# Last cross attention: K and V of batch 0 moved behind the last expert tile, gates and part of a quantisation moved into the expert stage

## Chip, cores and metric

One core of one Trainium2 chip runs the whole program. The metric is the time of one execution on the device, in microseconds (us); of several executions the median is given. A row of the trace gives a start and a duration from the first instruction of the profiled execution.

## What is computed

The reference is two transformer layers over 32 batches of 112 rows of 256 numbers, with a context of 375 rows of 192 numbers per batch:

```python
x = x + L0_xattn(layernorm(x), ctx)   # 16 heads of 16
x = x + L0_ffn(layernorm(x))          # self attention, then a mixture of 8 experts, 2 per row
x = x + L1_xattn(layernorm(x), ctx)   # 8 heads of 64
x = x + L1_ffn(layernorm(x))          # row blocks of 32 rounded to a 6-bit grid, times a rounded 256x256 weight
```

The part that matters here is where the experts end and the third line begins. Each row is sent to its two best experts, `moe_out = g0*y0 + g1*y1`, and the two gates are a softmax of the two best router logits, so `g0 = 1/(1+r)` and `g1 = r/(1+r)` with `r = exp(top1 - top0)`. In the last cross attention `k = ctx @ Wk` and `v = ctx @ Wv` need the context and the weights alone, while `q = layernorm(x) @ Wq` needs x, with the experts' result in it.

## The kernel before

The program has four parts that run one after the other on all engines: `cross_first`, `self_attention`, `experts`, `cross_last`. Every engine has its own list of instructions, in an order written out by hand, and waits on semaphores; the lists of the parts follow one another without a barrier.

**Experts (lines 1230 to 1450).** The rows were scattered by expert into `slots` in device memory, in 63 tiles of 128 rows (`MOE_TILES`). For each tile, SP loads `xg` and the first weight; TensorE turns `xg` (L1431), forms `hidden` (16 matmuls, L1423) and later the result `ps_out` (24 matmuls, L1443); ScalarE applies Gelu (L1338) and rounds the activations (`e_aH`, L1343) and the second weight (`e_w2H`, L1330); VectorE forms the low halves `e_aL` (L1394) and `e_w2L` (L1369, two halves) and adds the bias (`e_y`, L1389); SP stores `e_y` to `slots` (L1307). TensorE's order in step t is: hidden of t, turn of t+1, result of t-1. VectorE's order is: `e_xT` of t+1, `e_y` of t-1, `e_aL` and both halves of `e_w2L` of t.

In the step of the last tile VectorE also runs the first 3 of 13 steps (`EARLY`) that round the last weight `e_wf` (function `quantise_steps`, L1207 to L1222), and the other 10 behind the last `e_y`.

**Preparation in the expert stage.** In step 1, SP loads the contexts of batches 0 and 1, and the weights of `cross_last` (`preload`). ScalarE rounds Wk and Wv (L1524, L1526). GpSimd (POOL) splits the context of batch 0 into `c_cH` (L1576) and `c_cL` (L1582), and the low parts of Wk and Wv (L1592 to L1600). It then waits for the last store of the experts, and fetches the two expert rows of each row of batch 0 with two indirect DMAs into `c_got` (`fetch`, L1557 to L1567).

**Last cross attention (lines 1453 to 2142).** `step(b)` is written once per engine and unrolled for the first batches, then looped (`over_batches`, L56). The units in TensorE's order are: turn of the normalised rows `c_xn` (L1889), scores of head pairs 0 and 1 (L102, three split matmuls per head), q of the next batch (L1874), scores 3 and 2, values (L114) of the batch before, K of the next batch (four products of five matmuls, L182), V of this batch (three products of five), and turns of the probabilities (L108). Each K product goes through ScalarE twice (copy `c_kT`, rounded `c_kH`), and through GpSimd once (`c_kL`). VectorE mixes the expert rows into x (`mix`, L1774), takes moments (L155, L158), GpSimd forms the inverse deviation (L162, L164), and VectorE applies it (`c_xn`, L169). On VectorE the order is: mix of batch n, apply of batch n-1, moments of batch n.

At the start of this part VectorE and ScalarE form the gates (L1756 to L1762 and L1649). SP, in its step b (L1534 to L1544), waits until the context of batch b is split (`c_split`), then loads the context of batch b+2; in steps 0, 1 and 2 it also brings a third of the `residual` rows that were lent to the experts back from device memory (L1541).

`experts` calls, all in hand-written order:

```python
quantise = quantise_steps(dve, link, wf, wf, mx, 2 * D // MX, 128)
EARLY = 3
```

## Time and profile before

| what | value |
|---|---|
| median of 3 runs | 1969.74 us (1966.71 to 1970.39) |
| profiled execution, its own time | 1969.25 us |
| span of its instructions | 1967.4 us |
| outside the span | 1.85 us |
| TensorE busy | 1872.3 us (95%) |
| VectorE, ScalarE, GpSimd busy | 1495.6, 1270.8, 953.1 us |
| mean granted TensorE clock | 0.977 |
| expert stage | about 848 to 1288 us |
| last cross attention | about 1288 us to the end |

A view of the trace is read by time: a row has a start, a duration, the engine, the line of the kernel, `out<-in`, and in square brackets how long that engine was idle before it, and which instruction ended the idle time. PEld is TensorE's loading of weights, SPq and POOLq are queues that issue DMAs. In a table of stretches, each engine has its busy time and its count of instructions, and then come granted clock (1.00 is 2.4 GHz, 0.50 is 1.2 GHz), the DMA engines' mean share and GB/s.

### The profile page before, as it was taken

The numbers are of one execution on the slowest core, as the hardware profiler recorded it, in microseconds if no ns is written. First come the engines' busy times: TensorE is split into PE (matmuls) and PEld (weight loads), VectorE is DVE, ScalarE is ACT, GpSimd is POOL, SyncE is SP. The second block draws the span as 40 slices with busy tenths as digits, with TensorE's granted clock in tenths as the row PEclk, the third lists the DMA queues.
The fourth block names the chain that finished last, engine by engine and source line by source line (L and its number), as shares of the span: only waits on it lengthen the run. The fifth ranks groups of instructions, "written<-read, shape, count | busy, mean of one in ns | idle before, by whom it ended". The sixth has DMA issues, their size and how long they took to land.

```text
span 1967.4 us, 61539 instructions
## 1 busy us (share of the span) xinstructions
PE 1872.3 (95%) x20887; PEld 1642.5 (83%) x20887; DVE 1495.6 (76%) x3438; ACT 1270.8 (65%) x2720; POOL 953.1 (48%) x1616
## 2 busy tenths in 40 slices
PE   7999999999699999879999999969999999999996
PEld 5888888888578788679999999958888888888885
DVE  6778878887278887756766666657888888888886
ACT  2555555555377777657777777747777777777773
POOL 4566556655246766640000000057766767676751
PEclk9999999999799999889999999979999999999998
DMA  8222332231050111165565555421111111111100
GB/s 236 90 88 87 109 95 87 87 111 40 1 182 28 37 40 36 61 237 190 187 202 197 188 205 194 160 82 55 36 41 34 40 34 30 42 32 40 34 15 10
DMA packets 116596, 182.05 MB, mean 93 GB/s; under 512 B 10851, under 2 KB 94563, under 8 KB 116067
## 3 DMA queue, kind: packets, MB, share of 16 engines
q1 hardware_dynamic: 110386, 166.51, 26.6%
q0 software_dynamic: 6144, 14.69, 2.5%
q8 instruction: 40, 0.66, 0.1%
q14 instruction: 26, 0.21, 0.0%
HBM read 127.68 MB, written 53.48 MB: 92 GB/s over the span
## 4 chain that ended last, share of the span: by engine, by line
PE 52%; DVE 2%; issue 1%; ACT 1%; POOL 1%; DMA 0%; DVEq 0%; ACTq 0%; POOLq 0%; SPq 0%
PE ps_quad L1423 11%; PE ps_out L1443 9%; PE ps_quad L182 6%; PE ps_quad L102 4%; PE ps_out L114 4%; PE ps_turned L108 4%; PE ps_quad L1874 3%; PE ps_turned L182 3%; PE ps_proj L1894 3%; PE ps_proj L182 2%; PE ps_proj L1899 1%; DVE c_negmax L119 1%; PE ps_proj L1431 1%; ACT c_probs L134 0%; DVE e_w2L L1369 0%
## 5 line engine op out<-in xcount | busy, mean ns | idle before, releaser
L1423 PE MATMUL ps_quad<-e_xT,w 128*128 128x128 f32 x2016 | 235.3, 275 | 1.7 <-DVE e_xT L1381 1.7
L1423 PEld LDWEIGHTS ps_quad<-e_xT,w 128*128 128x128 f32 x2016 | 230.4, 192 | 2.2 <-DVE e_xT L1381 2.2
L364 ACT ACTIVATE a_probsT<-ps_quad 125x1792 f32<-125x1792 f32 x96 | 159.9, 1666 | 100.6 <-PE ps_quad L533 100.6
L1563 POOL TENSOR_TENSOR c_held<-minus_half 1x1 f32<-1x1 f32 x32 | 9.4, 294 | 410.8 <-DMA slots<-e_y 408.3
L1338 ACT ACTIVATE e_act_T<-ps_quad,fc_b 128x128 f32<-128x128 f32 x504 | 137.3, 384 | 94.2 <-PE ps_quad L1423 94.2
L134 ACT ACTIVATE c_probs<-ps_quad,c_negmax 112x375 f32<-112x375 f32 x256 | 143.8, 572 | 64.6 <-DVE c_negmax L119 64.6
L1443 PE MATMUL ps_out<-e_w2H,e_aH 128*128 128x256 f32 x504 | 149.1, 296 | 8.9 <-DVE e_w2L L1369 8.9
L126 DVE TENSOR_SCALAR c_probs<-c_probs,c_recip 112x375 f32<-112x375 f32 x256 | 151.5, 632 | 4.5
L1369 DVE TENSOR_TENSOR e_w2L<-w,e_w2H 128x1024 fp32r<-128x1024 f32 x126 | 151.4, 1243 | 0.0
L421 DVE TENSOR_REDUCE a_negmax<-ps_turned 112x2 f32<-112x750 f32 x128 | 120.1, 938 | 34.2 <-PE ps_turned L519 34.0
L119 DVE TENSOR_REDUCE c_negmax<-ps_quad 112x2 f32<-112x750 f32 x128 | 113.9, 930 | 40.0 <-PE ps_quad L102 39.5
L1443 PE MATMUL ps_out<-e_w2L,e_aH 128*128 128x256 f32 x504 | 143.1, 284 | 0.0
L1443 PE MATMUL ps_out<-e_w2H,e_aL 128*128 128x256 f32 x504 | 142.8, 283 | 0.0
L419 DVE TENSOR_REDUCE a_negmax<-ps_quad 112x4 f32<-112x1500 f32 x64 | 110.2, 1722 | 36.3 <-PE ps_quad L519 36.3
L1330 ACT ACTIVATE e_w2H<-w 128x1024 fp32r x126 | 125.6, 1042 | 2.5 <-PE ps_out L1443 2.5
L1389 DVE TENSOR_TENSOR e_y<-ps_out,e_b 128x256 f32<-128x256 f32 x63 | 26.7, 425 | 109.5 <-PE ps_out L1443 109.5
L1443 PEld LDWEIGHTS ps_out<-e_w2H,e_aH 128*128 128x128 f32 x504 | 97.0, 192 | 12.2 <-issue 6.1
L108 PEld LDWEIGHTS ps_turned<-ident,c_probs 112*125 112x125 f32 x768 | 100.9, 188 | 7.5 <-issue 2.4
L108 PE MATMUL ps_turned<-ident,c_probs 112*125 112x112 f32 x768 | 103.8, 271 | 1.8 <-ACT c_probsT L130 1.8
L130 ACT ACTIVATE c_probsT<-ps_turned 125x672 f32<-125x672 f32 x128 | 95.1, 743 | 10.6 <-PE ps_turned L108 8.2
L359 ACT ACTIVATE a_kT<-ps_proj,a_bk 128x376 f32<-128x376 f32 x64 | 36.8, 575 | 100.5 <-PE ps_proj L182 100.5
L1394 DVE TENSOR_TENSOR e_aL<-e_act_T,e_aH 128x1024 fp32r<-128x1024 f32 x63 | 78.3, 1243 | 30.3 <-issue 26.6
(350 smaller groups left out, 6025.1 us busy)
## 6 DMA issues: line engine op xcount, KB each, us to landing
w<-in_fc_t SPq DMA_DIRECT2D x71, 1024.0 KB, 4.9
slots<-a_zeros SPq DMA_DIRECT2D x60, 512.0 KB, 4.9
a_cT<-in_ctx_t SPq DMA_DIRECT2D x32, 375.0 KB, 3.5
c_cT<-in_ctx_t SPq DMA_DIRECT2D x32, 375.0 KB, 3.2
e_xg<-slots SPq DMA_DIRECT2D x63, 128.0 KB, 3.9
slots<-e_y SPq DMA_DIRECT2D x63, 128.0 KB, 1.8
out<-c_fo SPq DMA_DIRECT2D x32, 112.0 KB, 1.9
residual<-in_x SPq DMA_DIRECT2D x1, 2912.0 KB, 20.7
```

What stands on the lines that cost most here:

```text
L108: last = pe.transpose(self.turned[:, j, c * T:(c + 1) * T], self.probs[u][:, j, c * self.chunk:(c + 1) * self.chunk], ident[0:T, 0:T])
L119: dve.tensor_reduce(self.negmax[:, u, :], self.scores[u % 2], AX, ALU.max, negate=True).then_inc(self.max_ready, 1)
L126: last = dve.tensor_scalar(p, p, self.recip[:, u, j:j + 1], None, ALU.mult)
L134: last = act.activation(self.probs[u][:, j, :], self.scores[u % 2][:, j, :], ACT.Exp, bias=self.negmax[:, u, j:j + 1], accum_out=self.sums ...
L182: last = pe.matmul(dst, left, right, start=(i == 0), stop=(i == len(terms) - 1))
L364: act.activation(probsT[:, 2 * i:2 * i + 2, :, :].rearrange("p c r x -> p r c x"), quad[0:KC, :, 0:2 * HALF].rearrange("p r (c x) -> p r c ...
L421: dve.tensor_reduce(rows[:, 2 * half:2 * half + 2, 0], plain[0:T, :, 0:CTX], AX, ALU.max, negate=True)\
L1330: act.activation(w2H[:, half * HALF:(half + 1) * HALF], weights_half(e, half), ACT.Copy).then_inc(w2_high, 1)
L1338: last = act.activation(act_T[par][:, c * TILE:(c + 1) * TILE], hidden[par][:, c // 4, (c % 4) * TILE:(c % 4 + 1) * TILE], ACT.Gelu, bias= ...
L1369: dve.tensor_tensor(w2L[:, half * HALF:(half + 1) * HALF], weights_half(e, half), w2H[:, half * HALF:(half + 1) * HALF], ALU.subtract)\
L1423: last = pe.matmul(hidden[par][:, c // 4, (c % 4) * TILE:(c % 4 + 1) * TILE], mem["w1"][:, par, k, c * 128:(c + 1) * 128], xT[par][:, k, : ...
L1443: last = pe.matmul(y_ps[:, 0:D], left[:, rows], right[:, cols], start=(c == 0 and i == 0), stop=(c == NCH - 1 and i == 2))
```

## The change

Gates: the difference is taken before the first expert tile, and the three operations behind the exponential sit behind the first `e_xT`. Quantisation: `EARLY = (4, 7)`: four steps go ahead of the second-last `e_y`, three follow the last `e_w2L`, six stay behind the last `e_y`. K and V of batch 0: all seven products are issued behind the last expert result, before the turn of `e_wf`; ScalarE handles them in `first_products`; GpSimd forms the low parts in `first_low`, and splits the context of batch 1 in the expert stage. `later(b)` removes the same work for batch 0 from `step`. SP's list isn't edited.

```diff
 # experts, scalar
+                act.wait_ge(gap, 1)
+                act.activation(ratio[:, :], ratio[:, :], ACT.Exp).then_inc(ratioed, 1)
...
 # experts, vector
+                dve.tensor_tensor(ratio[:, :], mem["top"][:, :, 1], mem["top"][:, :, 0], ALU.subtract).then_inc(gap, 1)
...
-                EARLY = 3
+                EARLY = (4, 7)
...
+                    if isinstance(t, int) and t == MOE_TILES - 1:
+                        dve.wait_ge(bias_in, 32)
+                        for action in quantise[:EARLY[0]]:
+                            action()
                     if exists(t - 1, MOE_TILES):
...
+                    if isinstance(t, int) and t == -1:
+                        gates()
                     if isinstance(t, int) and t == MOE_TILES - 1:
-                        dve.wait_ge(bias_in, 32)
-                        for action in quantise[:EARLY]:
+                        for action in quantise[EARLY[0]:EARLY[1]]:
                             action()
...
 # cross_last
+        later = lambda b: not (isinstance(b, int) and b == 0)
...
 # cross_last, gpsimd
                 pool.wait_ge(v_split, 2)
+                context_high(1, 1)
+                context_low(1, 1)
                 index_rows(0, 0)
                 for i, tiles in enumerate(((MOE_TILES + 1) // 2, MOE_TILES // 2)):
                     pool.wait_ge(mem["y_out"][i], 16 * tiles)
                 fetch(0, 0)
+                fetch(1, 1)
+
+                def first_low(of):
+                    pool.wait_ge(k_high, 4)
+                    for tile in of:
+                        pool.tensor_tensor(kL[0][:, tile, :], kT[:, tile, :], kH[0][:, tile, :], ALU.subtract).then_inc(k_ready, 1)
+
+                first_low((0, 1))
...
                     if exists(b + 3):
                         norm.pool_rstd(pool, b + 3)
+                    if isinstance(b, int) and b + 3 == 0:
+                        first_low((3, 2))
...
 # cross_last, scalar
-                act.wait_ge(gap, 1)
-                act.activation(ratio[:, :], ratio[:, :], ACT.Exp).then_inc(ratioed, 1)
+                act.activation(unit[:, :], mem["eps"][:, :], ACT.Exp)
+                def first_products():
+                    k_from = (psum["turned"][:, 1, :], psum["quad"][:, 2, :], psum["quad"][:, 3, :], psum["turned"][:, 0, :])
+                    for at, tile in enumerate((0, 3)):
+                        act.wait_ge(k_mm, at + 1)
+                        act.activation(kT[:, tile, :], k_from[tile][:, 0:CTXE], ACT.Copy).then_inc(k_whole, 1)
+                    act.wait_ge(k_whole, 1)
+                    act.activation(kH[0][:, 0, :], kT[:, 0, :], ACT.Copy).then_inc(k_high, 1)
+                    act.wait_ge(v_mm, 1)
+                    act.activation(v[0][:, 2, :], proj[0:KC, 0:INNER], ACT.Copy).then_inc(v_ready, 1)
...
 # cross_last, vector
-                dve.tensor_tensor(ratio[:, :], mem["top"][:, :, 1], mem["top"][:, :, 0], ALU.subtract).then_inc(gap, 1)
...
-                dve.tensor_tensor(mem["gates"][1][:, :], mem["gates"][0][:, :], ratio[:, :], ALU.mult).then_inc(gated, 1)
...
 # cross_last, tensor
+                pe.wait_ge(c_split, 2)
+                pe.wait_ge(mem["experts_xT"], MOE_TILES)
+                pe.wait_ge(mem["experts_h"], MOE_TILES)
+                k_product(psum["turned"][:, 1, :], 0, 0)
+                k_product(psum["turned"][:, 0, :], 0, 3)
+                pe.wait_ge(v_split, 2)
+                v_product(proj, 0, 2)
+                k_product(psum["quad"][:, 3, :], 0, 2)
+                k_product(psum["quad"][:, 2, :], 0, 1)
+                v_product(psum["quad"][:, 0, :], 0, 0)
+                v_product(psum["quad"][:, 1, :], 0, 1)
                 pe.wait_ge(mem["last_y"], MOE_TILES)
                 pe.wait_ge(mem["wf_ready"], 1)
...
+                pe.wait_ge(v_ready, 3)
```

GpSimd's list behind the split of the weights, before and then after. `c_got` is filled by `fetch`, `c_kL` is the low half of K, `c_norm_rstd` the inverse deviation of the rows of one batch.

```order
L1600 TENSOR_TENSOR c_wvH<-c_wv,c_wvH 64x512
L1554 COPY c_index<-slot 112x1 x2
L1563 TENSOR_TENSOR c_held<-minus_half 1x1
L1565 DMA c_got<-slots,c_index 112x256 x2
...
L162 TENSOR_TENSOR c_norm_rstd<-c_norm_moments,eps 112x1
L164 TENSOR_TENSOR c_norm_rstd<-c_norm_rstd,minus_half 112x1
...
L1629 TENSOR_TENSOR c_qL<-c_qT,c_qH 128x448
L1634 TENSOR_TENSOR c_kL<-c_kT,c_kH 128x376
```

```order
L1620 TENSOR_TENSOR c_wvH<-c_wv,c_wvH 64x512
L1594 TENSOR_TENSOR c_held<-minus_half 1x1
L1596 CAST c_cH<-c_cT 128x376 x2
L1602 TENSOR_TENSOR c_cL<-c_cT,c_cH 128x376 x2
L1574 COPY c_index<-slot 112x1 x2
...
L1633 TENSOR_TENSOR c_kL<-c_kT,c_kH 128x376 x2
L162 TENSOR_TENSOR c_norm_rstd<-c_norm_moments,eps 112x1
L164 TENSOR_TENSOR c_norm_rstd<-c_norm_rstd,minus_half 112x1
L1633 TENSOR_TENSOR c_kL<-c_kT,c_kH 128x376 x2
```

The split of batch 1's context now stands ahead of the wait for the experts' last store, and two of the four low halves of K stand ahead of the first inverse deviation, the other two ahead of the fetch for batch 2.

TensorE's list from the last expert matmul on, before and then after. `ps_turned` and the first `ps_quad` rows are K, `c_wvH` marks V, `e_wf` is the last weight, `c_wq` is q.

```order
L1443 MATMUL ps_out<-e_w2H,e_aL_52 128x256
...
L1857 MATMUL ps_out<-ident,e_wf 128x128 x4
L1889 MATMUL ps_proj<-ident,c_xn 128x112 x2
L1874 MATMUL ps_quad<-c_xT,c_wq 128x112 x8
L182 MATMUL ps_turned<-c_cH,c_wkH 128x376
L182 MATMUL ps_turned<-c_cL,c_wkH 128x376
```

```order
L1463 MATMUL ps_out<-e_w2H,e_aL_52 128x256
...
L182 MATMUL ps_turned<-c_cH,c_wkH 128x376
L182 MATMUL ps_turned<-c_cL,c_wkH 128x376
...
L182 MATMUL ps_quad<-c_wvH,c_cL 125x512
L1954 MATMUL ps_out<-ident,e_wf 128x128 x4
L1926 MATMUL ps_proj<-ident,c_xn 128x112 x2
L1911 MATMUL ps_quad<-c_xT,c_wq 128x112 x8
```

The 35 matmuls of K and V stand before the turn of `e_wf`; in the stage of the first two batches they are gone.

## Rows read from the trace of the kernel before

**Rows 1.** Table of stretches: busy time and count by engine, clock, DMA share, GB/s.

```profile
868.00:882.00 14.00, 10.71 (x91) 10.04 (x90) 11.68 (x10) 9.57 (x19) 12.97 (x13) 1.00 0.80 267
...
1288.00:1300.00 12.00, 1.08 (x4) 0.73 (x5) 10.37 (x26) 0.83 (x2) 7.62 (x13) 0.58 0.55 158
...
1334.00:1352.00 18.00, 18.00 (x157) 16.31 (x151) 9.89 (x29) 13.68 (x35) 12.26 (x20) 1.00 0.29 87
```

**Rows 2.** Timeline of TensorE from the last expert tile to batch 1.

```profile
1295.08 1.08 PE L1857 MATMUL ps_out<-ident,e_wf 128*128 128x128 f32 x4 [7.32 <-DVE e_wf L1222]
1300.01 0.61 PE L1889 MATMUL ps_proj<-ident,c_xn 112*128 112x112 f32 x2 [3.85 <-DVE c_xn L169]
1301.07 3.75 PE L1874 MATMUL ps_quad<-c_xT,c_wq 128*128 128x112 f32 x16 [0.45 <-ACT c_xT L1750]
...
1309.43 0.43 PE L102 MATMUL ps_quad<-c_kH,c_qH 64*112 64x376 f32 x2
...
1312.61 0.43 PE L102 MATMUL ps_quad<-c_kH,c_qH 64*112 64x376 f32 x2 [2.41 <-POOL c_kL L1640]
...
1313.32 3.35 PE L1874 MATMUL ps_quad<-c_xT,c_wq 128*128 128x112 f32 x16
...
1323.39 0.47 PE L182 MATMUL ps_quad<-c_wvH,c_cH 128*125 128x512 f32 x1
...
1325.78 0.81 PE L108 MATMUL ps_turned<-ident,c_probs 112*125 112x112 f32 x6
...
1329.87 2.01 PE L1874 MATMUL ps_quad<-c_xT,c_wq 128*128 128x112 f32 x16 [1.00 <-ACT c_probs L134]
```

**Rows 3.** Timeline of VectorE around the mix of the first batches.

```profile
1296.32 1.13 DVE L1774 SCALAR_TENSOR_TENSOR residual<-c_got,gate,residual 112x256 f32<-112x256 f32 x2 [0.20 <-DMA c_got<-slots,c_index]
...
1299.06 0.48 DVE L1774 SCALAR_TENSOR_TENSOR residual<-c_got,gate,residual 112x256 f32<-112x256 f32 x1 [0.56 <-DMA c_got<-slots,c_index]
...
1304.57 0.41 DVE L169 TENSOR_SCALAR c_xn<-residual,c_norm_moments,c_norm_rstd 112x256 f32<-112x256 f32 x1
```

**Rows 4.** The first indirect DMA for batch 0, on GpSimd, and its landing.

```profile
L1565 POOL DMA_INDIRECT c_got<-slots,c_index x1: 1383/1383/1383, 1290.8 to 1290.8; - x1
...
DMA to landing us min/median/max: 5.4/5.4/5.4
```

**Rows 5.** The second indirect DMA for batch 1, on GpSimd, and its landing.

```profile
L1565 POOL DMA_INDIRECT c_got<-slots,c_index x1: 937/937/937, 1296.4 to 1296.4; - x1
...
DMA to landing us min/median/max: 2.6/2.6/2.6
```

**Rows 6.** Waits of SP's DMA queue from 1250 to 1330 us: total, times, longest.

```profile
SPq L1537 <- POOL c_cL L1582: 27.4, 1, 27.4
```

**Rows 7.** Timeline of GpSimd: low halves of q and of K, and both halves of a context.

```profile
1306.09 1.15 POOL L1629 TENSOR_TENSOR c_qL<-c_qT,c_qH 128x448 fp32r<-128x448 f32 x1 [2.82 <-ACT c_qH L1686]
...
1312.59 0.93 POOL L1576 CAST c_cH<-c_cT 128x376 fp32r<-128x376 f32 x2
1313.49 0.97 POOL L1610 TENSOR_TENSOR c_kL<-c_kT,c_kH 128x376 fp32r<-128x376 f32 x1
...
1315.37 1.91 POOL L1582 TENSOR_TENSOR c_cL<-c_cT,c_cH 128x376 fp32r<-128x376 f32 x2
```

**Rows 8.** Timeline of ScalarE in the first batches.

```profile
1311.88 0.57 ACT L134 ACTIVATE c_probs<-ps_quad,c_negmax 112x375 f32<-112x375 f32 x1
...
1318.70 0.58 ACT L134 ACTIVATE c_probs<-ps_quad,c_negmax 112x375 f32<-112x375 f32 x1 [0.84 <-DVE c_negmax L119]
...
1322.58 0.61 ACT L1718 ACTIVATE c_v<-ps_proj 125x512 f32<-125x512 f32 x1
...
1323.66 0.73 ACT L130 ACTIVATE c_probsT<-ps_turned 125x672 f32<-125x672 f32 x1
```

**Rows 9.** Timeline of VectorE in the first expert tiles, with and without GpSimd at work.

```profile
869.82 5.55 DVE L1369 TENSOR_TENSOR e_w2L<-w,e_w2H 128x1024 fp32r<-128x1024 f32 x2
...
887.30 2.35 DVE L1369 TENSOR_TENSOR e_w2L<-w,e_w2H 128x1024 fp32r<-128x1024 f32 x2
```

98 lines of the change are left out of this document (55 added, 43 removed).

## The prediction

> **What bounds the kernel now.** I read the table of stretches first, then TensorE's timeline through the border between the experts and the last cross attention, and then for each gap on TensorE the engine that ended it. In the expert stage and from 1334 us on TensorE is busy all the time: 18.00 of 18.00 us in the stretch from 1334 to 1352 [rows 1]. So time is won or lost only where TensorE stands idle, or runs at its lower clock, and the border is such a place: between 1288 and 1300 it is busy for 1.08 of 12.00 us [rows 1].
>
> Who ends these gaps? The first one, 7.32 us, ends when the last step of the quantisation has written `e_wf`; but behind the four short turns of `e_wf` TensorE waits again, 3.85 us, for `c_xn` of batch 0 [rows 2]. So the quantisation isn't the limit: `c_xn` is. VectorE's order is mix of batch 1, then apply of batch 0, and that mix ended its wait at 1299.06 on a gather [rows 3], which had been issued at 1296.4 and took 2.6 us to land [rows 5]. The front end of the stage is thus a chain of store, four gathers on GpSimd one after the other, mix, apply, turn at 1300.01, q at 1301.07. Behind it the pipeline fills: scores of batch 0 start at 1309.43, the second pair waits 2.41 us for a low half of K from GpSimd and starts at 1312.61, q of batch 1 starts at 1313.32, V has TensorE from 1323.39 to the turn at 1325.78, and q of batch 2 starts at 1329.87 [rows 2]. Behind that TensorE is full, and what is won until then stays won.
>
> **The change, part by part.** I say what each part does to the start of that last turn of batch 0 (1325.78, "the second turn"), because from there on the order of the work is the same.
>
> *Gates and quantisation: nothing.* They leave VectorE's list in front of the first mix, but that mix ended its wait on a DMA at 1296.32 [rows 3]: the gather for it was issued at 1290.8 and took 5.4 us, to 1296.2 [rows 4]. The gather covers them. If that cover were gone, the mix of batch 1 would still wait for its own gather. The four steps that now stand ahead of the second-last `e_y`, and the gates at the start, fall into VectorE's waits there; I put 0 on them.
>
> *K and V of batch 0 behind the last expert tile: cheap where they go.* Of the 35 matmuls, ten of V take 2.39 us [rows 2]; K's have fewer columns, so 35 last at most 8.4 us. They fill a gap of 7.32 us and part of the next, and end by about 1296, so the turn of `e_wf` isn't late, and `c_xn` comes long after.
>
> *From the turn to the first scores.* Before, this lasted from 1300.01 to 1309.43, 9.42 us [rows 2]. K is out of it now, but q, its copies on ScalarE and its low half are not: the low half ended at 1306.09 + 1.15 = 1307.24 [rows 7], so 7.2 us remain. Gain 2.2 us. There is a floor under it: the turn of batch 1 stands ahead of the first scores on TensorE, its rows were ready at 1304.57 + 0.41 [rows 3], and GpSimd now has four low halves of K (0.97 each [rows 7]) ahead of the fetch for batch 2. That fetch, and with it these rows, come some 3 us later, at 1308. So the first scores can't start before about 1308.7, whatever q does.
>
> *The gathers get company: a loss of 2.0 us.* SP's list isn't edited, but what it waits for moves. Before, SP stood for 27.4 us until the context of batch 1 was split [rows 6], and only then loaded the next context and brought the second third of `residual` back. Now that split is done in the expert stage, so SP issues both pairs of transfers in one go at about 1289 to 1290. The gathers of batch 0, which ran beside one such pair, took 5.4 us; those of batch 1, which ran beside nothing, 2.6 [rows 4, 5]. The two gathers of batch 1 will now run beside the second pair. The bounds are 0 and 2.8 us; I take 2.0, nearer to the row with company: the first pair kept the gathers until 1296.2, a second pair of the same size is at work for as long again, but the last gather, issued at 1296.4, meets only its second half. The Trainium skill (DMA: Bandwidth & Descriptors, "Queues, rings and completion order") says that a DMA engine takes turns between its queues packet by packet. By that rule the small packets of a gather wait behind one large packet each, for as long as the other queue has any, and the loss would be the whole 2.8.
>
> So `c_xn` of batch 0 is turned at about 1302.0 and the first scores start at 1302.0 + 7.2 = 1309.2, a gain of 0.2 us over 1309.43. The gather and the K work cancel.
>
> *From the first scores to q of batch 1: gain 0.7.* The wait of 2.41 us is gone, since both low halves are there. But q of batch 1 also waits for the exponentials of the first pair, in its place in PSUM. They ended at 1311.88 + 0.57 = 1312.45 [rows 8], 3.0 us behind the start of the scores, and at the lower clock I add 0.3: 1312.5, and with the handover 1312.6, against 1313.32 [rows 2].
>
> *From q of batch 1 to the second turn: gain 2.0 more.* The exponentials of the next pair started at 1318.70, 5.4 us behind q, and the copy of the first turned probabilities at 1323.66, 5.0 us behind that [rows 8]. Of these 5.0 us one copy of V (about 0.5 net of overlap, 0.61 in its row [rows 8]) is gone. So this copy starts at 1312.6 + 5.4 + 4.5 = 1322.4 (rounded down, as VectorE has less company from GpSimd) and ends with its 0.73 at 1323.1. Before, the second turn then had to wait until 1325.78 because V held TensorE; now it starts at 1323.1. In all the ramp gains 2.7 us. Of 7 us of TensorE's work only this much comes back, because ScalarE's chain of copies and exponentials is late next.
>
> *The clock.* q of batch 1 took 3.35 us and q of batch 2 the same work in 2.01 [rows 2]: the first at 1.2 GHz, the second at 2.4 GHz. Before, that q came after a busy stretch with a hole. Now TensorE is idle from about 1296 to 1302, and between the short pieces up to 1312.6, so I expect the lower level for both q products, as before. Were it the higher one, q of batch 1 would give 1.3 us more.
>
> *GpSimd's split of batch 1 in the expert stage: a loss of 0.8 us.* This is the hidden price. It adds 0.93 + 1.91 = 2.8 us of GpSimd work [rows 7], right behind its preparation at 868 to 882. There GpSimd was busy for 12.97 us, VectorE's two `e_w2L` took 5.55 us instead of 2.35 [rows 9], and TensorE was idle for 14.00 - 10.71 = 3.3 us at full clock [rows 1]; TensorE doesn't make that up, as it is the bound there. In proportion, 2.8 us more cost 3.3 / 12.97 x 2.8 = 0.7, and with the small instruction ahead of it 0.8. The bounds are 0 (all of it between VectorE's long instructions) and 2.8 (one for one). The Trainium skill (SBUF — State Buffer, "Who interferes with whom") says that a VectorE instruction with two inputs in SBUF and a GpSimd instruction that reads SBUF exclude each other, each for its whole length. By that rule the two splits and two casts hit only the instructions they meet, one of them off the path, and the sum would be nearer to 0.5.
>
> **Sum.** -2.7 + 0.8 = -1.9 us. The profiled execution took 1969.25 us, 0.49 below the median of 1969.74; its span is 1967.4 and 1.85 lie around it, untouched. From the profiled execution the sum gives 1967.35, from the median 1967.8. I predict the median to move alike: **1967.8 us**.
>
> **Rivals.** What a measurement of this kernel can tell from no change is about 0.2%, 3.9 us: the line is at 1965.8 and at 1973.7.
>
> 1. *The forecast*: the gathers cost what K gives, ScalarE is late next. 1967.8. Chance 0.5.
> 2. *The clock rises early and the gathers aren't disturbed.* The first scores then start at the floor, 1308.7 or earlier by a little, 0.7 us better with the handovers; q of batch 1 runs at 2.4 GHz, 1.3 us better; the expert stage loses nothing, 0.8 us better. That is -4.7 us: 1965.0. For it speaks that K and V keep TensorE busy up to 1295; against it the hole of 6 us behind. If VectorE, with fewer waits on the port, is also faster in the ramp, it goes lower. Chance 0.22.
> 3. *The expert stage is hit one for one, slower than before.* GpSimd's extra instructions come just as VectorE wants `e_aL` and the first `e_w2L`, on which TensorE waits. Price up to 2.8 us; with the gathers at their full 2.8 (0.8 more than in the sum) the total is -2.7 + 2.8 + 0.8 = +0.9 us: 1970.6. The point from which it decides: 2.7 us lost on TensorE between 880 and 895. `e_w2L` at more than twice its length [rows 9] speaks for it; against it, that only two of its instructions are long. To be slower by over 0.2% it takes a stall that hits several tiles. Chance 0.13.
> 4. *The change takes nothing off the path.* The two low halves ahead of the first inverse deviation, and the fetch behind the other two, make GpSimd the bound of the fill, and the second turn stays where it was. Then only the 0.8 remains: 1970.5. For it speaks that GpSimd has hardly a pause there in the old order [rows 7]; against it, that 2.8 us of splitting leave that same stretch. Chance 0.15.
>
> **Numbers.** The range should leave 2 in 10 out: from case 2, 1965.0, less 0.6 for it going lower, to case 3, 1970.6, with 0.2 for the spread of runs: 1964.4 to 1970.8. Faster by over 0.2% is most of case 2 and the lucky end of case 1: 0.24. Slower by over 0.2% is the far end of cases 3 and 4: 0.06. Within 0.2%: 0.70.
>
> **What would show it.** Right: in the profile after, K and V stand on TensorE behind the last expert result with no wait; SP issues two loads of context and two of `residual` within 2 us; the gathers of batch 1 land after more than 4 us; the first scores start as long after the last `e_y` as before, give or take 1 us; q of batch 1 takes over 3 us; the second turn comes 2 to 3.5 us earlier against that `e_y`; and the last `e_y` is itself 0 to 1.5 us later. Wrong: gathers of batch 1 that land in 2.6 us with both pairs of transfers in flight (the DMA term), q of batch 1 in 2 us (the clock), or a last `e_y` that is later by over 2 us (the port).

## The result and the profile after

| | before | after |
|---|---|---|
| median of 20 runs each | 1968.67 us (1962.82 to 1970.64) | 1972.15 us (1967.38 to 1978.09) |
| ratio, with its 95% interval | | 1.0016 [1.0008, 1.0023] |
| profiled execution, its own time | 1969.25 us | 1969.04 us |
| its span, mean granted clock | 1967.4 us, 0.977 | 1967.2 us, 0.977 |

The change made the kernel slower by 0.16%, some 3.1 us (0.0016 x 1968.67), where the forecast was 1.9 us faster: the time lies outside the range, and the direction is wrong. One execution in the whole study, 6886.47 us of the changed kernel in changed_again below, stands apart from all others, and the ratio there leaves it out.

The two profiled spans are equal by chance: the profiled execution after lies 3.1 us under its own median. The first hidden matmul of the experts started at 848.39 us after and at 852.21 before, and over all profiles of this study that start varied from 848.4 to 855.2 us. So I read stretches, each from a mark of its own. The marks in the ramp (the stretch from the last expert matmul to q of batch 2) are counted from the moment at which the last expert matmul makes room for what follows, its start plus 0.12 us, the pace of the matmuls ahead of it (1287.60 before, 1285.15 after). I call it the end of the last expert matmul:

| from the last expert matmul to the start of ... | before | after | forecast |
|---|---|---|---|
| the turn of `c_xn` of batch 0 | 12.41 | 18.22 | 14.4 |
| the first scores | 21.83 | 25.35 | 21.6 |
| q of batch 1 | 25.72 | 28.52 | 25.0 |
| the second turn of batch 0 | 38.18 | 39.43 | 35.5 |
| q of batch 2, the end of the ramp | 42.27 | 43.59 | 39.6 |

The forecast column is the prediction's own times less 1287.6. Its marks after the first turn were right: from the turn to the scores 7.13 us (7.2 forecast), from there to q of batch 1 3.17 (3.4), to the second turn 10.91 (10.5). The turn itself is 3.8 us later than forecast, and what follows adds only 0.2 us.

TensorE's timeline in the profile after, against [rows 2]:

```profile
1285.15 0.34 PE L182 MATMUL ps_turned<-c_cH,c_wkH 128*128 128x376 f32 x1
...
1291.84 0.40 PE L182 MATMUL ps_quad<-c_wvH,c_cL 128*125 128x512 f32 x1
1292.08 0.60 PE L1954 MATMUL ps_out<-ident,e_wf 128*128 128x128 f32 x4
1303.37 0.61 PE L1926 MATMUL ps_proj<-ident,c_xn 112*128 112x112 f32 x2 [10.69 <-DVE c_xn L169]
...
1310.50 0.43 PE L102 MATMUL ps_quad<-c_kH,c_qH 64*112 64x376 f32 x2 [1.42 <-POOL c_qL L1661]
...
1313.67 3.73 PE L1911 MATMUL ps_quad<-c_xT,c_wq 128*128 128x112 f32 x16 [1.50 <-ACT c_probs L134]
...
1324.58 0.88 PE L108 MATMUL ps_turned<-ident,c_probs 112*125 112x112 f32 x6 [1.18 <-DVE c_probs L126]
```

K and V run without a wait, in 6.9 us, and the turn of `e_wf` follows at once. Then TensorE is idle for 10.69 us in one piece, on `c_xn`. VectorE's timeline, against [rows 3], and GpSimd's in the same stretch:

```profile
1297.32 0.48 DVE L1817 SCALAR_TENSOR_TENSOR residual<-c_got,gate,residual 112x256 f32<-112x256 f32 x1 [7.20 <-DMA c_got<-slots,c_index]
1298.95 0.48 DVE L1817 SCALAR_TENSOR_TENSOR residual<-c_got,gate,residual 112x256 f32<-112x256 f32 x1 [1.15 <-DMA c_got<-slots,c_index]
...
1300.03 1.04 DVE L1817 SCALAR_TENSOR_TENSOR residual<-c_got,gate,residual 112x256 f32<-112x256 f32 x2
1301.22 2.00 DVE L169 TENSOR_SCALAR c_xn<-residual,c_norm_moments,c_norm_rstd 112x256 f32<-112x256 f32 x1
```

```profile
1300.61 0.58 POOL L164 TENSOR_TENSOR c_norm_rstd<-c_norm_rstd,minus_half 112x1 f32<-112x1 f32 x1
1301.17 1.90 POOL L1633 TENSOR_TENSOR c_kL<-c_kT,c_kH 128x376 fp32r<-128x376 f32 x2
...
1303.82 1.01 POOL L1585 DMA_INDIRECT c_got<-slots,c_index  x1 [0.17 <-issue]
```

Two delays stand one behind the other. The first mix starts 12.17 us behind the last expert matmul, 8.72 before. Then `c_xn` takes 2.00 us instead of 0.41: it starts 0.05 us behind a pair of low halves of K on GpSimd and ends just after it.

The first mix alone isn't the chain, though. The second mix waits again, for the second gather of batch 0, and behind it stand the moments, the inverse deviation on GpSimd (ready at 1301.19) and `c_xn` at 1301.22. Against the last expert matmul `c_xn` starts 4.2 us later than before (16.07 against 11.86) and takes 1.6 us more: together the turn's 5.8 us. The row of before:

```profile
1299.46 0.41 DVE L169 TENSOR_SCALAR c_xn<-residual,c_norm_moments,c_norm_rstd 112x256 f32<-112x256 f32 x1
```

Why the mix is late is in SP's queue, and in the DMA view of 1286 to 1300 us (size in KB, then median us to landing):

```profile
1286.43 0.43 SPq L1557 DMA_DIRECT2D c_cT<-in_ctx_t  x1
1286.90 0.49 SPq L1561 DMA_DIRECT2D residual<-kept_rows  x1
1287.44 0.43 SPq L1557 DMA_DIRECT2D c_cT<-in_ctx_t  x1
1287.91 0.47 SPq L1561 DMA_DIRECT2D residual<-kept_rows  x1
```

```profile
residual<-kept_rows SPq DMA_DIRECT2D x2, 896.0 KB, 8.9
c_cT<-in_ctx_t SPq DMA_DIRECT2D x2, 375.0 KB, 5.5
slots<-e_y SPq DMA_DIRECT2D x1, 128.0 KB, 1.7
c_got<-slots,c_index POOLq DMA_INDIRECT x4, 8.3
```

SP's wait of 27.4 us [rows 6] is gone, and both pairs are issued within 2 us, all of them before GpSimd's first gather goes out at 1288.21. The first gather lands after 9.0 us, against 5.4 [rows 4]; the other three take 9.1, 7.6 and 6.5 us, against 3.9, 2.6 and 2.6:

```profile
L1585 POOL DMA_INDIRECT c_got<-slots,c_index x1: 1317/1317/1317, 1288.2 to 1288.2; - x1
...
DMA to landing us min/median/max: 9.0/9.0/9.0
```

The table of stretches, for the 12 us that begin 0.40 us behind the last expert matmul in each trace (before: 1288 to 1300 in [rows 1]), shows both sides of it: TensorE is busy for 7.13 us instead of 1.08, at a granted clock of 1.00 instead of 0.58, and the DMA engines' share goes from 0.55 to 0.89.

```profile
1285.55:1297.55 12.00, 7.13 (x38) 6.15 (x36) 4.63 (x8) 5.83 (x12) 6.93 (x10) 1.00 0.89 249
```

And in the expert stage, on GpSimd, VectorE and TensorE:

```profile
877.91 3.79 POOL L1602 TENSOR_TENSOR c_cL<-c_cT,c_cH 128x376 fp32r<-128x376 f32 x2
```

```profile
876.83 4.01 DVE L1384 TENSOR_TENSOR e_w2L<-w,e_w2H 128x1024 fp32r<-128x1024 f32 x2
```

```profile
878.97 0.39 PE L1463 MATMUL ps_out<-e_w2H,e_aH 128*128 128x256 f32 x1 [2.00 <-DVE e_w2L L1384]
```

The added split meets the third tile's `e_w2L`. The split takes twice its undisturbed time (3.79 against 1.91 [rows 7]), `e_w2L` 1.7 times (4.01 against 2.35 [rows 9]), and TensorE waits 2.00 us, where the kernel before waited 1.18 at the same tile:

```profile
882.03 0.39 PE L1443 MATMUL ps_out<-e_w2H,e_aH 128*128 128x256 f32 x1 [1.18 <-DVE e_w2L L1369]
```

### The profile page after: what moved, and what is told of

It reads as the page before. It is cut to its first block, busy times and chain, and to the rows that moved or that the text cites. A ratio compares the mean times of both kernels' runs of the same rounds, so it can differ in the third digit from the quotient of the medians.

```text
span 1967.2 us, 61540 instructions
## 1 busy us (share of the span) xinstructions
PE 1868.0 (95%) x20887; PEld 1637.3 (83%) x20887; DVE 1498.4 (76%) x3438; ACT 1269.2 (65%) x2721; POOL 950.5 (48%) x1616
## 4 chain that ended last, share of the span: by engine, by line
PE 89%; DVE 4%; ACT 3%; issue 2%; DMA 1%; POOL 0%; DVEq 0%; ACTq 0%; POOLq 0%; SPq 0%
PE ps_quad L1443 11%; PE ps_out L1463 9%; PE ps_proj L182 9%; PE ps_quad L182 6%; PE ps_quad L533 5%; PE ps_quad L102 4%; PE ps_out L114 4%; PE ps_turned L108 4%; PE ps_out L541 3%; PE ps_quad L1911 3%; PE ps_proj L1931 3%; PE ps_turned L182 3%; PE ps_proj L617 2%; PE ps_turned L1100 2%; PE ps_out L1153 2%
```

## The experiments

The kernel before ran beside each group of runs, with medians of 1968.61 to 1969.73 us. Marks in the ramp are again counted from the end of the last expert matmul. The diffs show the lines that matter.

### The two parts alone, and the change once more

First the change itself again:

> The changed kernel, timed beside the others. Two stretches are read in each trace: the expert stage (first hidden matmul to the end of the last expert result; 435.6 us before, 436.8 changed) and the ramp (from there to the start of q of batch 2; 42.1 us before, 43.6 changed). Theory 1 (three prices, all of moves in time: gathers beside SP's second pair of transfers some 3.5 us, c_xn of batch 0 blocked 1.6 us by low halves of K, expert stage 1.3 us): this kernel repeats 43.6 and 436.8 within 0.5 us and is 2 to 4 us slower than before. Theory 2 (the slower time is not in these stretches): the two stretches stay near before's in this trace, and it is slower all the same.

1970.83 us against 1969.01, ratio 1.0013 [1.0004, 1.0022]. Turn at 17.71, q of batch 2 at 43.93, `c_xn` 2.00 us, the first expert tiles with the same 4.01 us. The picture of the first profile repeats in the ramp; the expert stage took 437.9 us, 1.1 more than expected.

Gates and quantisation moved as in the change, nothing else:

```diff
-                EARLY = 3
+                EARLY = (4, 7)
...
+                    if isinstance(t, int) and t == -1:
+                        gates()
```

> The kernel before with the gates and the quantisation moved, and nothing else. Theory 1: worth nothing, the mix of batch 0 waits for its gather; ramp 42.3 within 0.4, time within 0.1% of before. Rival (VectorE's shorter list lets GpSimd issue its gathers sooner, and that sets the front): ramp 1 us shorter.

1968.90 against 1969.04, ratio 0.9999 [0.999, 1.0008]; q of batch 2 at 41.74, 0.5 us earlier than before, just outside the 0.4 expected. In the time this part costs and gives nothing that can be told from zero, as forecast.

The kernel before with the context of batch 1 split in the expert stage, nothing else. Two lines put the split there, and two conditions take it out of the ramp:

```diff
                 pool.wait_ge(v_split, 2)
+                context_high(1, 1)
+                context_low(1, 1)
                 index_rows(0, 0)
...
-                    if exists(b + 2) and not (isinstance(b, int) and b + 2 == 0):
+                    if exists(b + 2) and not (isinstance(b, int) and b + 2 <= 1):
                         context_low(b + 2, par)
...
-                    if exists(b + 3) and not (isinstance(b, int) and b + 3 == 0):
+                    if exists(b + 3) and not (isinstance(b, int) and b + 3 <= 1):
                         context_high(b + 3, 1 - par)
```

> The kernel before with the context of batch 1 split in the expert stage, and nothing else. Theory 1 (the split draws SP's second pair forward, onto the gathers): gathers of batch 0 land after 9 us, ramp 3 to 3.5 us longer than before's 42.3, third and fourth e_w2L pair near 880 us stretched, 3 to 4.5 us slower in all (0.15 to 0.23%). Rival (the loss of the changed kernel comes from K and V, not from the split): ramp at or under 42.3.

1972.52 against 1969.04, ratio 1.0012 [1.0003, 1.002]. No product of K or V was moved here, and the kernel is already as slow as the changed one. The first gather takes 8.7 us, the turn comes at 16.35, 3.9 later than before, with `c_xn` at its 0.41 us. So **moving the split costs 3.9 us at the turn**, and this edit alone loses as much as the whole change. That it does so through SP's transfers is shown by e8_split_sp_holds below, where a hold of SP brings the turn back to 12.67. q of batch 1 ran at 2.4 GHz here (2.04 us), and q of batch 2 came at 45.18, 2.9 us late.

### Putting each delay right by itself

The split taken back to its old place (with the two conditions of e7_split_only put back as well), the rest of the change kept:

```diff
-                context_high(1, 1)
-                context_low(1, 1)
                 index_rows(0, 0)
```

> The split of the context of batch 1 goes back to where it was before the change; K and V of batch 0 stay early. With it SP's second pair goes back too. Theory 1: expert stage back to 435.6 (1.2 us shorter than changed), e_w2L never over twice its length behind 880 us, gathers as in the run in which SP holds, ramp 39.5 to 40.5: together 2 to 3.5 us faster than before. Rival (GpSimd's three us of splitting are in the way in the ramp, which is why they were moved): ramp over 42 us, and GpSimd ends TensorE's waits there.

1968.65 against 1969.01, ratio 1.0003 [0.9994, 1.0012]: the loss is gone, but the gain of 2 to 3.5 us that I expected isn't there. q of batch 2 comes at 41.13, not at 39.5 to 40.5. The first gather lands in 5.3 us, yet the turn is at 15.49, 3.1 us later than before. VectorE shows why: the mixes now meet the first two low halves of K on GpSimd, and `c_xn` the other two.

```profile
1294.50 3.08 DVE L1815 SCALAR_TENSOR_TENSOR residual<-c_got,gate,residual 112x256 f32<-112x256 f32 x2 [3.51 <-DMA c_got<-slots,c_index]
1298.18 1.04 DVE L1815 SCALAR_TENSOR_TENSOR residual<-c_got,gate,residual 112x256 f32<-112x256 f32 x2
1299.37 2.00 DVE L169 TENSOR_SCALAR c_xn<-residual,c_norm_moments,c_norm_rstd 112x256 f32<-112x256 f32 x1
```

A mix pair takes 3.08 us instead of 1.08 and `c_xn` 2.00 instead of 0.41: 3.6 us of VectorE's time in all, of which 3.1 reach the turn. This is the low halves' price when no late gather hides the first part of it. GpSimd's own pairs aren't stretched by the meeting: 1.91 and 1.90 us.

Next, the split stays early, but SP doesn't send the second pair until batches 0 and 1 are mixed:

```diff
+                    if isinstance(b, int) and b == 1:
+                        sp.wait_ge(mixed, 4)
```

> SP waits until the rows of batch 1 are mixed before its second pair of transfers; nothing else is changed. Theory 1 (the second pair delays the gathers): the four gathers land within 5.4 us of their issue instead of 9, first scores 4 us earlier, ramp 39.5 us instead of 43.6, expert stage still 436.8; in all about 1 us faster than before. Rival (the small packets of the gathers are slow beside any pair, and the second one adds little): gathers of batch 0 still take 8 us or more, ramp over 42.5 us.

1968.68 against 1969.01, 1.0005 [0.9991, 1.0018]; turn at 15.5, q of batch 2 at 42.55. The first gather lands in 5.6 us, so the second pair was what delayed it. The expected ramp of 39.5 isn't reached, and the time isn't below that of the kernel before: the same 3 us by the low halves remain, which I had left out here too.

Only the low halves of tiles 3 and 2 moved, behind the fetch for batch 3:

```diff
+                    if isinstance(b, int) and b == -1:
+                        first_low((3, 2))
...
-                    if isinstance(b, int) and b + 3 == 0:
-                        first_low((3, 2))
```

> The two later low halves of K of batch 0 go behind the fetch for batch 3, so that nothing of GpSimd stands beside the apply of batch 0. Theory 1 (the apply was held by them): c_xn of batch 0 takes 0.4 us instead of 2.0, ramp 1.5 us shorter than the changed kernel's: 42.1. Rival (the apply is late anyway, since the fetch for batch 2 or the gathers set the first scores): c_xn takes 0.4 but the ramp stays within 0.5 us of 43.6.

1972.26 against 1969.01, 1.002 [1.0009, 1.0032]. `c_xn` takes 0.41 us and the turn comes at 16.81, 1.4 earlier than in the changed kernel, but of these 1.4 us only 0.6 are left at q of batch 2 (43.02), and the time isn't better. The gathers, up to 9.3 us, still hold the turn.

### Both put right

The split back in the ramp, and the four low halves behind the gathers and the inverse deviations:

```diff
                 fetch(1, 1)
-                first_low((0, 1))
...
                     if exists(b + 3):
                         norm.pool_rstd(pool, b + 3)
+                    if isinstance(b, int) and b == -2:
+                        first_low((0, 1))
```

> Context of batch 1 split where it was before, and all four low halves of K of batch 0 behind the mixes: two behind the fetch for batch 2, two behind the fetch for batch 3. Theory 1 (what is left of the loss is low halves of K on GpSimd beside VectorE's mix and apply): the two mixes of batch 0 take 1.1 us instead of 3.1, c_xn 0.4 instead of 2.0, first scores about 19 us behind the last expert result instead of 22.7, ramp 38 to 39 instead of 41.1 (before: 42.3), 3 to 4 us faster than before in all. Rival (ScalarE and the low clock take back what the front wins): first scores at 19, but ramp at 40.5 or more.

1966.56 against 1969.04, 0.9995 [0.9983, 1.0006]. Turn at 12.12, first scores 19.47, second turn 33.76, q of batch 2 at 37.93: the ramp is 4.3 us shorter than before. That is what K and V behind the experts are worth in the ramp. The median is 2.5 us lower, but the interval of the ratio still holds 1.

Then the hold of SP as well:

> The same, and SP also holds its first pair of transfers until batch 1 is mixed, so that the gathers have the DMA engines alone. Theory 1 (the last gather of batch 1 is issued late enough to be alone anyway): gathers of batch 0 land after 2.7 us instead of 5.4, but first scores and ramp within 0.5 us of the run without this hold. Rival (the first pair is a price in the kernel before as well): first scores 1.5 us earlier.

The hold stands in SP's step 0, and the rest is the kernel above. 1967.54 against 1969.04, 0.9999 [0.9987, 1.001]. The turn is only 0.4 us earlier (11.76), and the held transfers now meet the gathers for batch 2, one of which takes 7.6 us: first scores 21.01, q of batch 2 39.95. Both come later than without the hold, which neither theory had. A hold moves the collision.

Back to the kernel before, with the early split and a hold of SP:

> The kernel before, with the split of batch 1's context in the expert stage (as in e7_split_only) and with SP held in its step 1 until both expert rows of batches 0 and 1 are mixed, so that its second pair of transfers goes out behind the gathers. Nothing else of the change. Theory A (the early split costs through the transfers it lets loose): the gathers land in 5.4 and 2.6 us again, the turn of c_xn comes 12.4 us behind the last expert matmul (16.35 in e7_split_only, 12.41 before), q of batch 2 at 42.3 us or a little earlier, as 2.8 us of GpSimd's work are out of the ramp. The whole is then above the kernel before by the expert stage's price alone: 1.2 us, so 1970.2 us against 1969.0, where e7_split_only was 3.5 above. Theory B (the early split costs in the expert stage, through VectorE): the transfers matter little, and it stays at 1972 to 1972.5 us. Theory C (it costs nothing there): 1969.0 or below.

1969.66 against 1968.61, 1.0002 [0.9991, 1.0013]. The first gather lands in 5.0 us and the turn is at 12.67, as theory A says: with SP held, 3.7 of the 3.9 us that e7_split_only lost at the turn are gone. But the gather for batch 2 takes 6.8 us, and q of batch 2 comes at 43.63. The median speaks against theory B. The interval bounds what the early split costs in the expert stage but doesn't size it.

The kernel of e4_lows_behind_fetch again:

> The kernel of e4_lows_behind_fetch once more: the change, but with the split of batch 1's context where it was before, the first two low halves of K behind the inverse deviation of batch 1 and the other two in the next step of GpSimd. There q of batch 2 came 37.93 us behind the last expert matmul (42.27 before, 43.59 in the changed kernel), and the median was 1966.56 against 1969.04, with an interval of the ratio that still held 1. If the ramp's 4.3 us reach the end: q of batch 2 at 37.5 to 38.5 us again and 1965 to 1967 us, with both intervals together under 1. If what is won in the ramp is lost behind it: the ramp is as short, and the median is within 1 us of the kernel before.

1967.11 against 1968.61, ratio 1.0003 [0.999, 1.0017]. q of batch 2 at 37.61, 4.7 us earlier than before: the ramp's gain repeats. The median is 1.5 us lower, but no interval is under 1, as was expected of both together: eight times lie between 1964.7 and 1968.0 and four between 1971.9 and 1974.5.

The early split kept, with the low halves behind the gathers and a hold of SP:

> The changed kernel, its early split kept, with SP held in its step 1 until batches 0 and 1 are mixed (as e1_sp_holds) and the four low halves of K behind the gathers and inverse deviations (as e4_lows_behind_fetch). Against e9_lows_behind_again it differs by the place of the split: in the expert stage here, in the ramp there. Theory A: gathers land in 5.4 and 2.6 us, c_xn of batch 0 takes 0.41 us, q of batch 2 stands at 37 to 38.5 us, and the expert stage's price of 1.2 us stays: 1966.5 to 1968 us, 0.5 to 1.5 above e9_lows_behind_again. If the early split's price in the expert stage is larger than I read (2 us or more), it is 1969 us or above; if it is nothing, it equals e9_lows_behind_again or is 0.5 us below it.

1966.67 against 1968.61, 0.9992 [0.9976, 1.0009], from 1958.80 to 1977.22. Its profile is one of the long executions: the second turn is at 35.58, and q of batch 2 only at 44.97.

The same with a longer hold:

> As e10_all_three, with SP held in its step 1 until batch 2 is mixed too, instead of batch 1. In e10_all_three the second pair of transfers went out at 1300.4 us, and the first gather for batch 2 (issued at 1301.2) took 6.5 us, the turn of batch 1 waited for its mix, and later one pair of VectorE's c_probs took 6.98 us instead of 0.74 beside 5.7 us of GpSimd's work without a pause, which is in its profile alone. If the collision of gathers and transfers is what a held pair still costs: the gathers for batch 2 land in 2.6 to 2.8 us, the turn of batch 1 comes 18.0 to 19.2 us behind the last expert matmul (20.19 in e10_all_three, 18.48 and 19.02 with the split left in the ramp), the second turn at 33.5 to 34.5, q of batch 2 at 37.5 to 38.5, and the median at 1965 to 1967 us, below the kernel before. If the order of GpSimd's work with the split taken out stalls VectorE in general (c_probs or another instruction at 4 us or more within the first three batches): q of batch 2 at 41 us or later in spite of the earlier turn, and a spread of the times of over 10 us as in e10_all_three.

1968.74 against 1969.73, 0.9992 [0.998, 1.0004]. The gathers for batch 2 land in time and the second turn is at 34.69, yet q of batch 2 comes at 44.08. So the collision was mended, and something else took the gain.

### A stall of 6.2 us, in some executions

The changed kernel's own third profile (e15_changed_beside, below) has it too. VectorE, GpSimd and TensorE there:

```profile
1326.79 0.79 DVE L126 TENSOR_SCALAR c_probs<-c_probs,c_recip 112x375 f32<-112x375 f32 x2
1327.50 0.14 DVE L122 RECIPROCAL c_recip<-c_sums 112x2 f32<-112x2 f32 x1
1327.68 6.96 DVE L126 TENSOR_SCALAR c_probs<-c_probs,c_recip 112x375 f32<-112x375 f32 x2
1334.56 1.77 DVE L119 TENSOR_REDUCE c_negmax<-ps_quad 112x2 f32<-112x750 f32 x2
```

```profile
1327.73 0.93 POOL L1585 DMA_INDIRECT c_got<-slots,c_index  x1 [0.30 <-issue]
1328.68 1.00 POOL L1672 TENSOR_TENSOR c_kL<-c_kT,c_kH 128x376 fp32r<-128x376 f32 x1
...
1329.76 0.93 POOL L1596 CAST c_cH<-c_cT 128x376 fp32r<-128x376 f32 x2
1330.66 0.96 POOL L1640 TENSOR_TENSOR c_kL<-c_kT,c_kH 128x376 fp32r<-128x376 f32 x1
1331.59 0.96 POOL L1643 TENSOR_TENSOR c_kL<-c_kT,c_kH 128x376 fp32r<-128x376 f32 x1
1332.52 1.90 POOL L1602 TENSOR_TENSOR c_cL<-c_cT,c_cH 128x376 fp32r<-128x376 f32 x2
1334.39 0.29 POOL L162 TENSOR_TENSOR c_norm_rstd<-c_norm_moments,eps 112x1 f32<-112x1 f32 x1
```

```profile
1334.69 1.60 PE L108 MATMUL ps_turned<-ident,c_probs 112*125 112x112 f32 x6 [4.13 <-DVE c_probs L126]
...
1336.88 3.73 PE L1911 MATMUL ps_quad<-c_xT,c_wq 128*128 128x112 f32 x16 [0.59 <-ACT c_probs L134]
```

Two instructions that take 0.79 us a moment earlier take 6.96. The first of them starts 0.05 us ahead of GpSimd's indirect DMA and isn't the one that is held; the second starts 0.31 us behind it and takes 6.60 us:

```profile
1328.04 6.60 DVE L126 TENSOR_SCALAR c_probs<-c_probs,c_recip 112x375 f32<-112x375 f32 x1
```

It ends 0.2 us behind the last large pair on GpSimd, `c_cL`, while small instructions go on there. TensorE waits 4.13 us and pays again, since q of batch 2 then runs at 1.2 GHz (3.73 us against 2.01). The profiles of e10_all_three and e11_hold_longer show the same at 6.98 and 6.97 us, with the second instruction at 6.61 in both. Of eleven profiles of kernels with K and V moved and no guard against it, three have it, one of them the changed kernel's; none of the four with K and V left in the ramp does.

A shorter case stands in e4_lows_behind_fetch, on the first pair of batch 0, beside a pair of `c_kL` and the pair of `c_cL`, with no indirect DMA going out between them:

```profile
1309.09 3.91 DVE L126 TENSOR_SCALAR c_probs<-c_probs,c_recip 112x375 f32<-112x375 f32 x2
```

```profile
1308.66 1.91 POOL L1631 TENSOR_TENSOR c_kL<-c_kT,c_kH 128x376 fp32r<-128x376 f32 x2
1310.54 1.92 POOL L1602 TENSOR_TENSOR c_cL<-c_cT,c_cH 128x376 fp32r<-128x376 f32 x2
```

The guard is one wait on GpSimd, for the four normalised pairs of batch 0, behind the fetch and ahead of the next low half. First on e11_hold_longer, then on e9_lows_behind_again:

```diff
+                    if isinstance(b, int) and b == -1:
+                        pool.wait_ge(core.probs_ready, 4)
                     if exists(b + 2) and later(b + 2):
                         pool.wait_ge(k_high, 4 * b + 10)
```

> As e11_hold_longer, with one wait more: in the step in which GpSimd forms the last low half of K of batch 1, it first waits until VectorE has normalised all four pairs of batch 0. In e11_hold_longer that pair (c_probs) took 6.97 us beside GpSimd's 5.7 us of work without a pause. If that stall is what makes the upper half of the times: the pair takes 0.74 to 1.2 us, q of batch 2 stands at 37.5 to 38.5 us behind the last expert matmul (44.08 in e11_hold_longer) and takes 2.0 us, the times lose their upper half (highest under 1970), and the median falls by 3 to 4 us to 1965, with an interval of the ratio that ends below 1. If the stall only moves to VectorE's next instruction, or the clusters have another cause: the median stays at 1967 to 1969 and the spread at 12 us or more.

1967.16 against 1968.88, 0.9992 [0.9984, 1.0001], highest 1968.99 instead of 1974.01. The pair takes 0.74 us, q of batch 2 is at 37.47. The upper half of the times is gone, but the median didn't come down by the 3 to 4 us expected, and the interval ends just above 1.

> As e9_lows_behind_again (split of batch 1's context in the ramp, low halves behind the gathers, SP free), with GpSimd's wait for the four normalised pairs of batch 0 as in e12_pool_waits. In the profile of e9_lows_behind_again that pair was done 1.1 us before GpSimd's long stretch, so the wait costs nothing there. If the stall makes the upper cluster in the other executions: all times from 1964 to 1969, a median of 1965.5, and an interval of the ratio below 1. If not: four in twelve above 1971 as before, and a median of 1966.5 to 1967.5. Against e12_pool_waits it tells the early split's price in the expert stage once more: e12 above e13 by 0.5 to 2 us if it costs, equal if not.

**1965.28 against 1968.88, ratio 0.9975 [0.9964, 0.9986]**, highest 1968.93 instead of 1974.48. In seven executions this version beats the kernel before by 0.25%, and the changed one by more. Its profile, of the longest of the seven, has q of batch 2 at 39.04, so that all of the gain isn't seen in it. It differs from e12_pool_waits in the split's place and in SP's hold; its median is 1.9 us lower (mean 2.1, with a standard error of 1.2), which points to the early split's price in the expert stage and doesn't fix it.

What speaks for the guard is the spread. Of the 60 executions in the five runs with the low halves behind the gathers and no guard (e4, e5, e9, e10, e11) fifteen lie above 1971 us; of the 18 with it (e12, e13) none is above 1969. How it does it isn't shown: in no profile with the guard does GpSimd stand still at it, the low half behind it starts 0.02 to 0.03 us after the fetch in each.

The changed kernel beside the next one:

> The changed kernel itself. Both theories: 1970.8 to 1972.2 us, a spread of 8 to 10 us. If its profiled execution is one of the long ones (1973 us and up), the theory of the stall expects a pair of c_probs of 4 to 7 us within the first three batches in it; the rival expects none.

1971.91 against 1969.62, ratio 1.0015 [1.0005, 1.0026]. The profiled execution, 1977.51 us, is the longest, and shows the stall above, q of batch 2 at 48.80.

The guard in the changed kernel:

> The changed kernel with one wait more, GpSimd's for the four normalised pairs of batch 0, as in e12_pool_waits. If the stall of c_probs is in some executions of the changed kernel: its upper times (1973 to 1978 in 8 of 20) go, the highest is under 1972 us, and the median is 1969.5 to 1970.5 against some 1971.5 of e15_changed_beside. What is then left above the kernel before, 0.5 to 1.5 us, is the ramp (1.3 us later) and the expert stage. If the stall belongs only to the versions with the low halves behind the gathers: it equals e15_changed_beside within 1 us and keeps its spread of 9 to 10 us.

1972.24 against 1969.62, 1.0018 [1.0006, 1.0029], up to 1976.15: a miss. In the changed kernel the guard takes nothing away. Its profile shows no stall and q of batch 2 at 43.40.

One more profile of it:

> The kernel of e14_changed_pool_waits again, for one more profile. If it is a short execution (span under 1971): no VectorE instruction of the first three batches over 4 us, q of batch 2 43 to 44 us behind the last expert matmul. If it is a long one (span over 1973) and the stall makes it long: some VectorE instruction of 4 us or more there in spite of the wait, and q of batch 2 at 47 us or later. If it is long with q of batch 2 at 43 to 44: the stall isn't what makes the long executions of this kernel.

A single time of 1967.28 us: a short execution, without the stall, q of batch 2 at 43.84. What makes this kernel's other long executions stays open.

## Why the prediction was wrong

**The gathers' company: the step that failed.** The prediction let the first gather of batch 0 land in 5.4 us as before and gave the second pair's cost to the gathers of batch 1 alone: 2.0 us, at most 2.8. But it had itself put both pairs on SP's queue in one go, and that is before GpSimd issues its first gather. So all four gathers stand beside 2.5 MB instead of 1.3, and the first two take 9.0 and 9.1 us. For the last gather the term was of the right size: it lands 14.3 us behind the last expert matmul, 2.9 later than before. But the two of batch 0, at nothing in the sum, land 3.5 and 5.0 us later, and behind the second of them VectorE still has a mix, the moments and both mixes of batch 1 to do. That sets the start of `c_xn`, 4.2 us late in the profile after. In e7_split_only, where nothing else is moved, it cost 3.9 us at the turn, and with SP held (e8_split_sp_holds) 0.3. The bound of 2.8 was too low because the 5.4 us of the first gather [rows 4] were taken as the price of company, when they were the price of one pair: against the 2.6 us of a gather alone, one pair cost the first gather 2.8 us, and two cost it 6.4. The rule of the Trainium skill (DMA: Bandwidth & Descriptors, "Queues, rings and completion order"), turns taken packet by packet, was the better guide in direction: the gathers wait as long as the other queue has packets. The trace agrees within 2 us: SP's last transfer lands at 1299.1 us, and the four gathers between 1297.2 and 1299.4. The full 2.8 that I drew from it was still short, as I applied it to the last gather only.

**The low halves beside VectorE: a step that was missing.** I counted the four low halves only as a delay of GpSimd's fetch. They also stretch what VectorE runs beside them, and that is on the path to `c_xn`: 1.6 us in the profile after (2.00 against 0.41), 3.1 to 3.6 us where the gathers are in time (e3_split_back, e1_sp_holds). The rule of the Trainium skill that I did cite for the expert stage (SBUF — State Buffer, "Who interferes with whom"), one engine blocks for the other's whole instruction, points at the mixes here, which have two inputs in SBUF. The trace goes beyond it: the 1.90 us on GpSimd are two instructions (0.96 us each), and `c_xn`, with one input from SBUF, is held over both.

**The expert stage: 0.8 forecast, 1.2 measured and not clear of zero.** From the first hidden matmul to the first of the tenth tile, twelve profiles with the early split took 64.3 to 68.6 us, mean 66.5, and seven without it 63.2 to 67.2, mean 65.4. The difference of 1.2 has a standard error of 0.7 (over the whole stage 1.0, with 0.6), for where GpSimd's work meets the tiles varies from run to run. The bounds of 0 and 2.8 hold.

**What held.** Gates and quantisation: nothing (e6_gates_only). K and V cost nothing where they stand. SP issues both pairs in one go. q of batch 1 runs at 1.2 GHz (3.73 us at a granted clock of 0.50). The prediction read the 3.35 us of before as the same level, but the granted clock there was 0.57, so a part of them ran at the higher one; the 0.4 us between the two are as much as the stretch to the second turn is over its term. From the turn on each stretch is within 0.4 us of its term. The 0.7 us that the prediction gives to the stretch up to q of batch 1 are the sum up to there, 0.2 of them from the stretch before. With both delays put right K and V give 4.3 to 4.7 us in the ramp; the forecast without its gather term is 4.7.

**The sum with measured terms.** Ramp +1.3 in place of -2.7, expert stage +1.2 in place of +0.8: +2.5, within the measured 3.1 [1.6, 4.5]. Rivals 3 and 4, the two on the slower side, had the right sign and the wrong place. Rival 3 set its point of decision in the expert stage, and the loss came in the gathers. Rival 4 named the low halves, but as work that makes GpSimd late, and not as what stretches VectorE; the first scores ended their wait on the low half of q, not on the fetch for batch 2. The stall was on nobody's list. In three profiles it put q of batch 2 9.4 us behind the second turn instead of 4.2, but by e14_changed_pool_waits it doesn't carry the changed kernel's median.

## What to carry to other kernels

Removing a wait from a queue also removes the spacing that it gave to what is behind it: write down what is issued at once then, and which transfers issued later, on another queue, must pass it. When work goes into an idle stretch, check what the neighbours on VectorE and GpSimd do in that stretch as well as the engine that it is for. And look at the spread of the times beside their median: a second cluster some 7 us up led to a stall that three of eleven profiles show, and with one wait against it a version that couldn't be told from before came out 0.25% faster, in seven executions and without a profile that shows the wait at work.

## What the runs showed of the hardware

- A gather of 112 rows on the indirect queue landed in 2.6 us alone, 5.4 beside one pair of transfers (1.3 MB), and 9.0 us beside two.
- VectorE's instructions that met low halves in the ramp took about the sum of both: `c_xn` 0.41 to 2.00 beside a pair of 1.90, a mix pair 1.08 to 3.08 beside one of 1.91, and GpSimd's pairs kept their length. In the expert stage both sides were stretched, VectorE's 2.35 us to 4.01 and GpSimd's 1.91 to 3.79.
- An instruction of VectorE can be kept out over several instructions on GpSimd in a row, not only for the one that it meets: 6.6 us in three profiles (a pair 6.96 to 6.98 us for 0.79 us of work), and a pair 3.91 us in e4_lows_behind_fetch. In the three long cases the pair had started 0.05 to 0.06 us ahead of an indirect DMA's issue on GpSimd. That this is the trigger is not shown: e13_behind_pool_waits has the same alignment with 0.77 us, and the case of 3.91 us has no such issue beside it.
